# Expert rows of a decoder layer: 16-bit halves by transposing transfers in place of TensorE transposes

## The reference, cut to what matters

```python
x = x + attention(layernorm(x))          # 8 heads, q and k RMS-normalised, B=2, N=2048, D=512
x = x + cross_attention(layernorm(x), ctx)   # 16 heads, 128 context rows
xn = layernorm(x)
idx = top_k(xn[:, 0, :] @ Wr + br, 2)    # 2 of 8 experts for each batch, by its first row
h = gelu(einsum('bsd,bkde->bkse', xn, W1[idx]) + b1[idx])
x = x + sum_k(einsum('bkse,bkef->bksf', h, W2[idx]) + b2[idx]) / 2
```

## Time and profile before

| | us |
|---|---|
| median of 3 runs | 2325.82 (2325.12 to 2328.04) |
| the profiled execution | 2321.48 |
| its span | 2319.6 |
| TensorE busy | 2189.6 (94%) |
| VectorE busy | 1565.5 (67%) |
| ScalarE busy | 1609.7 (69%) |
| GpSimd busy | 1483.9 (64%) |
| transfers, share of the 16 engines' span | 12.3% |

### The profile page before, as it was taken

How to read it: one execution, slowest core, us unless ns; L and a number is a source line. 1 busy time by engine, 2 the same in 40 slices (tenths; PEclk the granted TensorE clock), 3 DMA queues, 4 the chain that set the end, 5 groups by cost and what they waited for, 6 DMA issues and landing times. The chain is left out here.

```text
span 2319.6 us, 63272 instructions
## 1 busy us (share of the span) xinstructions
PE 2189.6 (94%) x22392; PEld 1256.9 (54%) x22392; DVE 1565.5 (67%) x2601; ACT 1609.7 (69%) x1831; POOL 1483.9 (64%) x980
## 2 busy tenths in 40 slices
PE   6998999999997989899999899999999978998999
PEld 3544666666665445444445446666666644554444
DVE  6987777777776756753379877777777766667532
ACT  4555999999998556731145579999999975566210
POOL 4324998989988577731233158898998976867210
PEclk9998999999999999999999989999999999999999
DMA  4210000000001301102122100000000022011000
GB/s 105 64 37 5 2 9 9 9 9 9 9 0 29 105 1 38 46 15 77 46 55 58 34 1 10 0 9 9 9 9 9 4 63 67 1 47 37 19 22 34
DMA packets 102338, 65.10 MB, mean 28 GB/s; under 512 B 75346, under 2 KB 75346, under 8 KB 102226
## 3 DMA queue, kind: packets, MB, share of 16 engines
q1 hardware_dynamic: 102226, 63.57, 12.3%
HBM read 46.69 MB, written 8.39 MB: 24 GB/s over the span
## 5 line engine op out<-in xcount | busy, mean ns | idle before, releaser
L751 POOL TENSOR_TENSOR probs_l<-wide 128x1024 f16<-128x1024 f32 x448 | 986.3, 2234 | 162.3 <-PE bank L803 120.7
L887 DVE TENSOR_REDUCE pm<-bank 128x1 f32<-128x512 f32 x1024 | 680.5, 688 | 249.1 <-PE bank L759 244.2
L878 ACT ACTIVATE wide<-bank,shift 128x1024 f32<-128x1024 f32 x512 | 570.4, 1114 | 37.3 <-DVE probs_l L901 30.7
L870 ACT ACTIVATE wide<-bank,shift 128x1024 f16<-128x1024 f32 x512 | 567.6, 1109 | 10.9 <-PE bank L775 10.9
L759 PE MATMUL bank<-ko,q_hh 128*128 (+1 forms) x1024 | 397.0, 390 | 22.3 <-PEq L454 12.2
L774 PE MATMUL bank<-q_hh,ko 128*128 (+1 forms) x1024 | 389.9, 381 | 18.1 <-ACT wide L878 13.1
L775 PE MATMUL bank<-q_lm,k_h 65*128 (+1 forms) x1024 | 389.8, 381 | 0.0
L788 PEld LDWEIGHTS bank<-v_hl,wide 128*128 128x128 f16 x4096 | 287.5, 98 | 63.4 <-issue 5.7
L788 PE MATMUL bank<-v_hl,wide 128*128 (+1 forms) x4096 | 319.8, 192 | 0.1
L790 PE MATMUL bank<-v_hl,wide 128*128 (+1 forms) x4096 | 318.0, 193 | 0.0
L790 PEld LDWEIGHTS bank<-v_hl,wide 128*128 128x128 f16 x4096 | 267.4, 96 | 58.7
(11 more groups left out here) (211 smaller groups left out, 4187.5 us busy)
## 6 DMA issues: line engine op xcount, KB each, us to landing
wide<-in_x SPq DMA_DIRECT2D x32, 256.0 KB, 2.6
q_lm<-in_x SPq DMA_DIRECT2D x32, 256.0 KB, 3.2
ko<-in_L_ffn_W SPq DMA_DIRECT2D x32, 256.0 KB, 3.8
q_hh<-q_hh SPq DMA_DIRECT2D x32, 128.0 KB, 2.6
ko<-k_h SPq DMA_DIRECT2D x32, 128.0 KB, 2.8
out<-bo_b SPq DMA_DIRECT2D x16, 256.0 KB, 2.0
out<-xbo_b SPq DMA_DIRECT2D x16, 256.0 KB, 2.0
q_lm<-nm SPq DMA_DIRECT2D x248, 0.2 KB, 4.9
```

Source lines behind the costliest of these rows:

```text
L751: pool.tensor_tensor(probs_l[:, p % 2, :], probs[:, p % 2, :], probs_h[:, p % 4, :], ALU.subtract).then_inc(pl_pool, 1)
L870: act.activation(probs_h[:, p % 4, :], SB[p % 2][:, :], ACT.Exp, bias=shift[:, 0:1]).then_inc(ph_ready, 1)
L878: act.activation(probs[:, p % 2, :], SB[p % 2][:, :], ACT.Exp, bias=shift[:, 0:1]).then_inc(p_ready, 1)
L887: dve.tensor_reduce(pm[:, s, k:k + 1], MB[k % 2], AX_X, ALU.max).then_inc(mx_free, 1)
```

## The change

For chunks 1 to 3 the t3 tiles no longer go through TensorE and PSUM. ScalarE's high copies the float32 tile as it lies in tokx to 16 bits into tokh[:, j % 2], VectorE's low writes the rest into tokl[:, j % 2], and SyncE issues two transposing transfers for each tile (128x512 16-bit elements, 128 KB), which write x2th and x2tl. high of tile j waits until the transfers of tile j − 2 have landed. SyncE's transfers stand in its queue: chunk 1's behind the first four weight pieces and the biases, ahead of the other four; chunk 2's behind those; chunk 3's two and two behind the stores of result(0, 0) and result(0, 1). TensorE's loop waits for the transfers' counts. VectorE's list swaps low t3(3, x) and result(0, x) in places. Chunk 0 stays as it was, since the routing reads it.

```diff
+                        tokh = sb(tp, "tokh", [P, 2, D], F16)
+                        tokl = sb(tp, "tokl", [P, 2, D], F16)
...
+                        def by_transfer(kind, c, j):
+                            return kind == "t3" and c >= 1
+
                         TILES = [turn for turn in T_TURNS if turn[0] != "sm"]
                         T_BASE = b * len(TILES)
+                        T_TURNS = [turn for turn in T_TURNS if not by_transfer(*turn)]
+                        PE_TILES = [turn for turn in T_TURNS if turn[0] != "sm"]
+                        PE_BASE = b * len(PE_TILES)
...
+                        def turned(c, j):
+
+                            return (b * 2 * (CH - 1) + (c - 1) * 2 + j // 2 + 1) * 32
...
+                            def turn(c, j):
+                                cols = slice((c * TPC + j) * P, (c * TPC + j + 1) * P)
+                                sp.wait_ge(d_tl, T_BASE + t_of("t3", c, j) + 1)
+                                sp.nop(nofuse=True)
+                                sp.dma_start_transpose(x2th[:, :, cols], tokh[:, j % 2, :]).then_inc(d_turned[j % 2], 16)
+                                sp.dma_start_transpose(x2tl[:, :, cols], tokl[:, j % 2, :]).then_inc(d_turned[j % 2], 16)
...
+                            for j in range(TPC):
+                                turn(1, j)
                             load_pieces(sp, b, PIECES_P4[4:], stage_f, src)
+                            for j in range(TPC):
+                                turn(2, j)
...
-                                    sp.wait_ge(d_t_done, T_BASE + len(TILES))
+                                    sp.wait_ge(d_tl, T_BASE + len(TILES))
...
                                     sp.dma_start(out_rows[bass.ds(n * CT + j * P, P), :], yt[j % 2][:, :])\
                                         .then_inc(y_out[j % 2], 16)
+                                    if c == 0 and j < 2:
+                                        turn(3, 2 * j)
+                                        turn(3, 2 * j + 1)
...
-                            transposes("t3", 1, 0)
...
-                            transposes("t3", 3, 1)
-                            transposes("t3", 3, 2)
-                            transposes("t3", 3, 3)
...
-                                pe.wait_ge(d_tl, T_BASE + t_of("t3", c, TPC - 1) + 1)
+                                for j in range(2):
+                                    pe.wait_ge(d_turned[j], turned(c, TPC - 1))
...
+                        def tile_src(kind, c, j):
+                            return tokx[c % 2][:, j, :] if by_transfer(kind, c, j) else tile_bank(kind, c, j)
+
                         def t_dst(kind, c, j, low):
 
+                            if by_transfer(kind, c, j):
+                                return (tokl if low else tokh)[:, j % 2, :]
...
-                                act.wait_ge(d_t_done, T_BASE + i + 1)
+                                if by_transfer(kind, c, j):
+                                    act.wait_ge(d_n1, n * TPC + j + 1)
+                                    if turned(c, j) > 32:
+
+                                        act.wait_ge(d_turned[j % 2], turned(c, j) - 32)
+                                else:
+                                    act.wait_ge(d_t_done, PE_BASE + pe_of(kind, c, j) + 1)
...
-                                act.activation(t_dst(kind, c, j, False), tile_bank(kind, c, j), ACT.Copy).then_inc(d_th, 1)
+                                act.activation(t_dst(kind, c, j, False), tile_src(kind, c, j), ACT.Copy).then_inc(d_th, 1)
...
-                                dve.tensor_tensor(t_dst(kind, c, j, True), tile_bank(kind, c, j),
+                                dve.tensor_tensor(t_dst(kind, c, j, True), tile_src(kind, c, j),
                                                   t_dst(kind, c, j, False), ALU.subtract).then_inc(d_tl, 1)
...
                             result(b * CH, 0, 0)
-                            result(b * CH, 0, 1)
                             low("t3", 3, 0)
                             low("t3", 3, 1)
+                            result(b * CH, 0, 1)
                             low("t3", 3, 2)
+                            low("t3", 3, 3)
                             result(b * CH, 0, 2)
                             result(b * CH, 0, 3)
-                            low("t3", 3, 3)
```

More of the change, by code:

```diff
@@ L273, in decoder_layer @@
         d_th = sem("d_th")
+        d_turned = [sem(f"d_turned{i}") for i in range(2)]
         d_tl = sem("d_tl")
@@ L1179, in _ @@
                                    "w20": rows_of(w2, expert[0]), "w21": rows_of(w2, expert[1])}
-                            sp.wait_ge(d_t_done, T_BASE + t_of("t5", CH - 1, TPC - 1) + 1)
+                            sp.wait_ge(d_t_done, PE_BASE + pe_of("t5", CH - 1, TPC - 1) + 1)
                             sp.nop(nofuse=True)
@@ L1747, in _ @@
                             scores(2, 2)
-                            transposes("t3", 1, 1)
                             query(3, 0)
@@ L1752, in _ @@
                             values(2, 4)
-                            transposes("t3", 1, 2)
                             maxima(3, 1)
@@ L1758, in _ @@
                             maxima(3, 3)
-                            transposes("t3", 1, 3)
                             scores(2, 3)
@@ L1788, in _ @@
                             cross_project(2, 2)
-                            transposes("t3", 2, 0)
                             cross_project(2, 3)
@@ L1792, in _ @@
                             values(3, 3)
-                            transposes("t3", 2, 1)
                             scores(3, 2)
@@ L1797, in _ @@
                             values(3, 4)
-                            transposes("t3", 2, 2)
                             values(3, 5)
-                            transposes("t3", 2, 3)
                             scores(3, 3)
@@ L1815, in _ @@
                             cross_project(3, 2)
-                            transposes("t3", 3, 0)
                             cross_project(3, 3)
@@ L1875, in layer_norm @@
                                 if s:
-                                    act.wait_ge(d_t_done, T_BASE + t_of("t2", c, j) + 1)
+                                    act.wait_ge(d_t_done, PE_BASE + pe_of("t2", c, j) + 1)
                                 elif c:
-                                    act.wait_ge(d_t_done, T_BASE + t_of("t0", c - 1, j) + 1)
+                                    act.wait_ge(d_t_done, PE_BASE + pe_of("t0", c - 1, j) + 1)
                                 act.activation(tokx[c % 2][:, j, :] if s else tok0[:, j, :], x2_tile(c, j), ACT.Identity,
@@ L2142, in _ @@
                                 if c == EARLY and not LAST:
-                                    act.wait_ge(d_t_done, T_BASE + len(TILES))
+                                    act.wait_ge(d_tl, T_BASE + len(TILES))
                                     act.wait_ge(f_b2, 2 * b + 2)
@@ L2266, in expert_raw @@
                                 if w == 0:
-                                    dve.wait_ge(d_t_done, T_BASE + t_of("t0", CH - 1, TPC - 1) + 1)
+                                    dve.wait_ge(d_t_done, PE_BASE + pe_of("t0", CH - 1, TPC - 1) + 1)
                                 elif w == 4:
-                                    dve.wait_ge(d_t_done, T_BASE + t_of("t3", CH - 2, TPC - 1) + 1)
+                                    dve.wait_ge(d_tl, T_BASE + t_of("t3", CH - 2, TPC - 1) + 1)
                                 dve.wait_ge(f1_done, b * (CH * 8) + w + 1)
```

2 lines of the change are left out of this document (added).

## The result

The changed kernel takes 2333.91 us (median of 19 runs, 2327.39 to 2340.98), the kernel before 2326.57 beside it (19 runs): a ratio of 1.0029, 95% interval 1.0021 to 1.0038, **6.7 us slower**. Measured once more with the experiments it was 1.0016 (1.0004 to 1.0028). In this text a ratio is turned into us by 2326: +6.7 and +3.7.

What follows compares the result with a forecast made beforehand. TensorE was taken as the bound, except where it waits for GpSimd and VectorE. Per batch −2.97 −0.43 +1.7 +1.2 = −0.5, twice −1.0, from 2325.82 to 2325 us; range 2314 to 2347, the forecast's own 2320 to 2329.

Steps and rivals of the forecast that it cites:

- slow transfers: Rival, chance 0.25: transposing transfers take 4.9 us each, one after the other, so tiles come late: 2345.
- port queue: Chunks 1 and 2: VectorE subtractions with two SBUF operands take turns with GpSimd: +1.7 and +1.2 us a batch.
- t3(3,0): Chunk 3's first tile, at 2165 in a full TensorE stretch: removing its transposes gives −0.43 us a batch.
- Tail of chunk 0: Between chunk 0's last expert_down and chunk 1's first expert_up: last three tiles' transposes and TensorE's idle go, −2.97 us a batch.
- t3(1,0): Chunk 1's first tile, in a full TensorE stretch ahead of scores(2,2): up to −0.43 us, booked with chunk 1.
- the further loss that hung on 0.15 us: Chunk 1: a line 176 also loses its turn to GpSimd's next subtraction; bound +3.4 us, not taken into the sum.
- The transfers' landing: Each transposing transfer takes 2.8 us to land and 0.8 to issue; a pair lands 3.6 us behind its subtraction.
- the 2 us to spare in chunk 2: Chunk 2: a pair of transfers has about 5.8 us before ScalarE is held, so it stays hidden.
- The loads of w2, "So 0": SyncE's w2 loads, behind chunk 1's transfers, land near 2108.5, hidden by ScalarE's idle 1.91 us: 0, at most +3.6.
- The rival of late weights: Chance 0.10: a transposing issue holds SyncE 2.6 us, w2 loads land 3.6 us later, +3.6 a batch: 2332.
- the seven tiles in waiting stretches: t3(1,1) to t3(2,3), where TensorE waits for GpSimd or VectorE: removing their transposes gains nothing.

Runs made afterwards that it cites:

- c2: The changed kernel, but TensorE still makes the transposes of chunks 1 and 2, into banks nobody reads: +6.5 us against the kernel before, clock 0.9768.

## Why the prediction was wrong

2325 with "same" was forecast, a change of −1.0; the time moved by +6.7, and by +3.7 when measured again. It is outside the forecast's own 2320 to 2329. That it lies inside 2314 to 2347 is luck: the range reaches so high for slow transfers, which did not come. Of the 7.7 us between −1.0 and +6.7, the late loads of w2 are about 5, the port queue's excess 1.3 and t3(3,0) 0.9. Step by step:

- **Tail of chunk 0, −2.97 a batch**: −2.98 in both batches, and −2.97 or −2.98 in every profile with chunk 3 by transfer. Right. t3(3,0)'s −0.43 is in no trace (6.82 to 6.80 across it). It was read as lying in a full stretch; behind it stood a wait for VectorE's low half of t2(3,3), which the transposes had covered.
- **t3(1,0), −0.43**: right, 0.43 in both batches.
- **The port queue**: the mechanism was right, low(1,2) blocked by line 1236 and all. Its size was 1.7 + 0.43 in chunk 1 and 1.2 in chunk 2, 6.7 us in all; the runs have 7.0, 7.2, 8.2 and 10.0. So the sum is somewhat small (by its own times output(2,5) is 1.8 later, not 1.7), and its parts lie otherwise: ahead of scores(2,3) the first profile has +1.08 and +1.09 where I had 2.1 (the further loss that hung on 0.15 us did not come), +1.0 ahead of scores(3,3) of batch 1, and behind each of them 1.1 to 1.6 as half clock, which I had not foreseen. The lock that the Trainium skill states in "SBUF — State Buffer", section "SBUF: two separate sides", agrees with all of these traces.
- **The transfers' landing**: right, 2.5 us for 2.8, though of the 2 us to spare in chunk 2, batch 0 kept 0.65 and batch 1 2.13. The slow rival is false. The Trainium skill's 1309 ns for a block ("VectorE: DVE Perf Modes", "The three transpose paths") would make 5.2 us of four blocks, and the rows have 2.5; its other rule, that one is as fast as an ordinary transfer ("Advanced Engine Details and Errata", "X-Bar Transpose (TRN2)") agrees with the landing.
- **The loads of w2, "So 0"**: this is the step that failed. It put at nothing a term that measures about 5 us. With the loads on time the changed kernel is 5.4 us faster by the means (2.5 side by side), and 3.5 and 6.3 in the other pairs. The working put the sixth load at 2108.5, 1 us inside the slack, with three terms too small. An issue took 1.2 us, not 0.8: +0.85 for a pair. The pieces come 2.3 us apart (2109.27, 2111.62, 2113.94) with the DMA engines full, share 1.01 at 242 GB/s from 2106 to 2110, where I had a median landing added to the last issue: from the first issue to t2(2,0) it is 10.4 us. And ScalarE's split of the last piece, 1.06, stands between load and t2(2,0), and was left out. In the first profile that shows as no more than +0.05 and +0.50 at the row maxima, since chunk 1 had become later by more than I gave it; in the second as +1.9 and +0.3. The rest may be clock in part, (0.9747 − 0.9733) × 2325 × 0.7 = 2.3 by the line; that is argued, not shown. The rival of late weights had the right place, at a price of 7 us for a 2.6 us issue that didn't come, and 0.10.
- **The clock** stands nowhere in the sum. "Nothing" for the seven tiles in waiting stretches took full speed behind the waits for granted. That is also why one trace against one trace misled: the profiled execution of before, at 0.982, was one with little loss. The half-clock stretches are part of how port queue and late loads cost what they cost, so they aren't added to them. What the changed kernel's lower mean clock is worth stays open: +8 us by the line, but c2, with most of that clock back, is no faster.

The sum with measured terms: tail −5.3 (chunk 3 alone), port queue about +8, late loads about +5, t3(1,0) −0.9: +6.8, against +6.7 and +3.7. The terms are differences of runs with ±3 us each, and the changed kernel itself is in one of them, so this closes no better than that.

Open: why loads held back in the kernel before cost nothing, while they cost 3.5 to 6.3 wherever transfers precede them. In the run with transfers and no port queue the row maxima are 2.0 and 3.1 us late, in the one with held loads, which start 1.8 us earlier, 0.5 and 1.2. Part of the answer may lie there; how much later a load may be was not varied.

## What to carry to other kernels

When a queue gets more issues, follow the transfers behind them to the last consumer: their pace at full DMA bandwidth and the consumer's own work, not one median landing. When work is taken out of a full stretch, look at what the next step waits for: that wait may have been covered by it. A hole at the end of a stage may be an order's fault; try the order before moving work to another unit. Where the clock wanders between executions, judge terms of a few us by runs, side by side, with the clock beside them, and don't turn a difference of clocks between two kernels into time by a line fitted within one: here a clock 0.003 lower went with no longer time.

## What was not expected of the hardware

- A transposing transfer of 128 x 512 two-byte elements from SBUF to SBUF held SyncE's queue for 1.20 to 1.26 us and landed in 2.5 (medians; most 2.32 and 5.4), as fast as the plain copy of the same size (2.6).
- Stretches at half clock shift between places from one execution of a kernel to the next; over the executions of the kernel before the mean granted clock ran from 0.975 to 0.983, and its time with it.
- With TensorE's waits filled by other work, one profile had clock 1.00 at the filled places and 0.50 at the next wait; the mean clock rose from 0.9733 to 0.9762, and the time did not fall.
